# Self-attention: the output projection for two pairs of heads in every odd step, instead of for eight pairs at a batch's end

## The reference

```
def _attn(xq, ctx, wq, wkv, wo, bo):
    q = _heads(xq @ wq)
    k, v = jnp.split(ctx @ wkv, 2, axis=-1)      # then rope on q and k
    sim = jnp.einsum('bhnd,bhmd->bhnm', q, k) * DH ** (-0.5)
    a = jax.nn.softmax(sim, axis=-1)
    o = jnp.einsum('bhnm,bhmd->bhnd', a, v)      # (b, n, 1024) after merging heads
    return o @ wo + bo

attn_in = _adaln(x, cond, ...)
x = _attn(attn_in, attn_in, sa_wq, sa_wkv, sa_wo, sa_bo) + x
x = _attn(_adaln(x, cond, ...), _ln(context, ...), ca_wq, ca_wkv, ca_wo, ca_bo) + x
x = ffn(x) + x
```

## Time and profile before

| | |
|---|---|
| median of 3 runs (lowest, highest) | 1942.67 us (1939.44, 1943.04) |
| profiled execution, its span | 1940.06 us, 1938.3 us |
| PE busy | 1886.2 us, 97% |
| DVE busy | 1573.7 us, 81% |
| POOL busy | 1266.3 us, 65% |
| ACT busy | 945.6 us, 49% |
| self-attention, first to last reciprocal (start) | 43.3 to 404.8 us |

### The profile page before, as it was taken

How to read it: one execution, slowest core, us unless ns; L and a number is a source line. 1 busy time by engine, 2 the same in 40 slices (tenths; PEclk the granted TensorE clock), 3 DMA queues, 4 the chain that set the end, 5 groups by cost and what they waited for, 6 DMA issues and landing times.

```text
span 1938.3 us, 52005 instructions
## 1 busy us (share of the span) xinstructions
PE 1886.2 (97%) x19952; PEld 1288.5 (66%) x19952; DVE 1573.7 (81%) x2292; ACT 945.6 (49%) x1460; POOL 1266.3 (65%) x816
## 2 busy tenths in 40 slices
PE   7989999988999999999999999999999999999999
PEld 5656766755666666666666666666666666666664
DVE  5998888867888888888888888888888888888852
ACT  3445554533544544444554444445544445554444
POOL 5777756415677667666766766776676676767652
PEclk9999999978999999999999999999999999999999
DMA  6322233201111111111111111111111111111110
GB/s 189 105 80 85 78 107 90 78 30 49 59 52 56 51 55 50 56 57 54 56 51 54 52 56 56 54 55 52 53 53 56 56 55 53 54 51 54 50 32 23
DMA packets 147729, 119.07 MB, mean 61 GB/s; under 512 B 63392, under 2 KB 111648, under 8 KB 147488
## 3 DMA queue, kind: packets, MB, share of 16 engines
q1 hardware_dynamic: 110624, 115.46, 17.9%
q10 hardware_dynamic: 36864, 0.28, 1.0%
HBM read 36.71 MB, written 1.05 MB: 19 GB/s over the span
## 4 chain that ended last, share of the span: by engine, by line
PE 86%; issue 3%; DVE 3%; DMA 3%; POOL 2%; SPq 1%; ACT 1%; ACTq 0%; DVEq 0%; POOLq 0%
PE S L1373 24%; PE OB L1387 20%; PE PB L1335 10%; PE PB L1322 9%; PE S L1354 7%; DMA swapped<-turned 2%; PE PB L1396 2%; PE PB L1307 2%; PE S L1224 2%; PE PB L1406 1%; PE PB L1270 1%; PE OB L1252 1%; PE OB L1235 1%; PE PB L1190 1%; DVE QK L966 1%
## 5 line engine op out<-in xcount | busy, mean ns | idle before, releaser
L708 POOL TENSOR_TENSOR psum_acc<-psum_acc,P 124x1024 f32<-124x1024 f32 (+1 forms) x320 | 689.8, 2156 | 214.7 <-ACT P L851 205.2
L851 ACT ACTIVATE P<-S 124x1024 f32<-124x1024 f32 (+1 forms) x448 | 431.3, 963 | 512.4 <-PE S L1373 512.3
L1068 DVE TENSOR_REDUCE mxc<-S 128x2 f32<-128x1024 f32 x384 | 470.0, 1224 | 91.4 <-PE S L1354 84.4
L1387 PE MATMUL OB<-P,V 124*64 124x256 f32 (+1 forms) x3328 | 436.0, 386 | 0.0
L1387 PEld LDWEIGHTS OB<-P,V 124*64 124x64 f32 (+1 forms) x3328 | 221.0, 136 | 187.6 <-issue 103.4
L701 POOL TENSOR_TENSOR psum_acc<-P 124x1024 f32<-124x1024 f32 x64 | 152.0, 2375 | 211.8 <-ACT P L851 208.3
L1373 PE MATMUL S<-QH,KH 64*124 64x256 f32 (+1 forms) x1664 | 272.0, 323 | 5.8 <-ACT P L851 5.8
L728 ACT ACTIVATE V<-PB 124x512 f32<-124x512 f32 (+1 forms) x320 | 157.2, 491 | 203.0 <-PE PB L1335 165.3
L1373 PEld LDWEIGHTS S<-QH,KH 64*124 64x124 f32 (+1 forms) x1664 | 154.1, 181 | 128.2 <-issue 104.3
L1373 PE MATMUL S<-QL,KH 64*124 64x256 f32 (+1 forms) x1664 | 235.1, 278 | 0.0
L1373 PE MATMUL S<-QH,KL 64*124 64x256 f32 (+1 forms) x1664 | 234.8, 278 | 0.0
(11 more groups left out here) (159 smaller groups left out, 2828.7 us busy)
## 6 DMA issues: line engine op xcount, KB each, us to landing
swapped<-turned SPq DMA_DIRECT2D x512, 128.0 KB, 2.1
kv_w<-sa_kv_dram SPq DMA_DIRECT2D x64, 128.0 KB, 2.3
qswapped<-qturned SPq DMA_DIRECT2D x128, 64.0 KB, 1.9
kv_w<-ca_kv_dram SPq DMA_DIRECT2D x64, 96.0 KB, 2.2
ctxT_all<-ctx_dram SPq DMA_DIRECT2D x8, 624.0 KB, 4.6
q_w<-sa_wq_dram SPq DMA_DIRECT2D x64, 64.0 KB, 2.0
q_w<-ca_wq_dram SPq DMA_DIRECT2D x64, 64.0 KB, 1.9
o_w<-ca_wo_dram SPq DMA_DIRECT2D x64, 64.0 KB, 2.0
```

The source lines that it names most:

```text
L708: pool.tensor_tensor(acc, acc, P_of(J, c)[0:rows, :, 0:w], ALU.add).then_inc(x.acc, 1)
L851: act.activation(P_of(J, c)[0:rows, :, 0:w], SP[0:rows, :, 0:w], ACT.Exp, scale=SCALE).then_inc(x.e, 1)
L1068: dve.tensor_reduce(mxc[:, t, :, c:c + 1], MP[:, :, 0:w], AX.X, ALU.max).then_inc(x.am, 1)
L1387: ins = pe.matmul(OB[half(h), 0:N], Vb[J % 2][0:w, t, half(h)], P_of(J, c)[0:w, h, k * N:(k + 1) * N], start=(t == 0), stop=(t == len(a_.t ...
```

## The change

`o` moves to the second place of PE's turn, between `qk` and `p`, and two steps behind instead of one. It now acts in every odd step J, in turn J + 2: four matmuls for the pairs J - 1 and J, as an accumulation of their own. `ad` goes two steps behind too, between `am` and `r`, and adds each such part to `xT`; the bias goes with the first part of a batch. There are 32 groups of 4 matmuls for 8 groups of 16, and 32 additions for 8. The semaphores `z.y` and `z.added` count to 32 instead of 8, and their waits are rewritten; the buffers `oTs` stay eight.

```
-                 "qk+3 ln+3 p+-1 sum+-1 v+2 s a+2 ct o+-1 n",
-                 "c+2 ln+2 am+1 r+2 t+3 rc+-1 dv+-1 ad+-1 cn n",
+                 "qk+3 ln+3 o+-2 p+-1 sum+-1 v+2 s a+2 ct n",
+                 "c+2 ln+2 am+1 ad+-2 r+2 t+3 rc+-1 dv+-1 cn n",
...
                 def divide(J, _):
-                    wait(dve, z.y, batch(J))
+                    wait(dve, z.y, (J - PAIRS) // 2 + 1)
...
                 def add(J, _):
-                    if J % PAIRS == PAIRS - 1:
-                        wait(dve, z.y, batch(J) + 1)
+                    if J % 2:
+                        wait(dve, z.y, J // 2 + 1)
+                        wait(dve, z.added, J // 2)
                         x_b = xT[:, batch(J) * N:batch(J) * N + N]
-                        add_to_x(x_b, XB[:, 0:N], 8).then_inc(z.added, 1)
+                        add_to_x(x_b, XB[:, 0:N], 8 if J % PAIRS == 1 else None).then_inc(z.added, 1)
...
-                           "o": (z.added, lambda K, k: batch(K) + 1 if K % PAIRS == PAIRS - 1 else None)}
+                           "o": (z.added, lambda K, k: K // 2 + 1 if K % 2 else None)}
...
                 def output(J, _):
-                    if J % PAIRS == PAIRS - 1:
-                        wait(pe, z.wo, 16 * PAIRS)
+                    if J % 2:
+                        if J == 1:
+                            wait(pe, z.wo, 16 * PAIRS)
                         wait(pe, z.ot, J + 1)
                         x_free(uses, readers, J, ("o", 0))
-                        for p in range(PAIRS):
+                        for p in (J % PAIRS - 1, J % PAIRS):
                             for h in range(2):
                                 ins = pe.matmul(XB[half(h), 0:N], o_w[p][:, half(h)], oTs[p][:, :],
-                                                start=(p == 0), stop=(p == PAIRS - 1))
+                                                start=(p % 2 == 0), stop=(p % 2 == 1))
                         ins.then_inc(z.y, 1)
```

More of the change, by code:

```diff
@@ L525, in cross_out_weights @@
                 if J < UNROLL:
-                    wait(sp, z.y, B)
+                    wait(sp, z.y, STEPS // 2)
                 sp.dma_start(o_w[r][:, :], packs["ca"][2][pair]).then_inc(x.wo[r], 16)
@@ L1239, in transposes @@
                         wait(pe, z.oe, J)
-                        wait(pe, z.added, 2)
+                        wait(pe, z.added, PAIRS)
                         first[FIRST[J]](0)
@@ L1328, in project_v @@
                     if J == 0:
-                        wait(pe, z.added, B)
+                        wait(pe, z.added, STEPS // 2)
                     x_free(uses, readers, J, ("v", g))
@@ L1419, in ramp_mean @@
                     if k == NLN - 2:
-                        pe.wait_ge(z.added, B)
+                        pe.wait_ge(z.added, STEPS // 2)
                     others["mean"](k)
```

## The result

| | before | changed |
|---|---|---|
| median (lowest, highest; executions) | 1942.59 us (1938.47, 1948.58; 16) | 1935.89 us (1930.89, 1938.40; 16) |
| profiled execution, its span | 1940.06, 1938.3 us | 1936.41, 1934.6 us |
| granted clock, mean over the executions | 0.989 to 0.990 | 0.987 |

The ratio is 0.9963 [0.9954, 0.9972], that is 7.2 us less (5.4 to 8.9). Forecast were 1932.5 us and 10.2 less.

What follows compares the result with a forecast made beforehand. DVE was taken to bound plain steps, PE those with transposes, both losing at batch ends. Terms -31.5 + 3.9 + 1.4 + 8.1 + 6.1 + 1.8 = -10.2 us, from 1942.67, gave 1932.5 us, range 1926 to 1941.

Steps and rivals of the forecast that it cites:

- the sum: Whole change: 31.5 us saved at batch ends, less the added costs of the stretches and turn 63, gives -10.2 us.
- signs of being wrong: Waits of 0.3 us before `v` or sums in many odd turns, fold releasing them, or self-attention gain that cross-attention doesn't keep.
- DVE decides: Steps 0 to 23 and 39 to 46: each odd turn costs 0.34 us for its addition, 3.9 and 1.4 us.
- The cover: Odd turns without transposes: PE's added matmuls are hidden, the sums ending a bare 0.1 us before DVE wants them.
- PE decides: Steps 23 to 39: eight odd turns cost 1.01 us each, 8.1 us against 9.0 saved.
- six paid groups: Steps 46 to 62: six odd-turn matmul groups at 1.01 us each cost 6.1 us against 9.0 saved.
- DVE's idle time: Before the additions: as a sign of being right, it falls from 28.7 us to under 3.
- Turn 63: Last self-attention sums wait for an addition queued behind cross-attention work; scores 2.0 us late, 1.8 us lost.
- The step that failed: Ramp into cross-attention: 12 fewer matmuls, 2.75 us of PE, counted as nothing because PE waits for DVE's maximum anyway.
- rival 2: Ramp: thinner PE work brings TensorE's lower clock some 6 us earlier, costing about 3 us: 1935.5; chance 0.13.
- Rival 3: Odd turns: a PE, DVE, PE round trip stalls each of 31 by 0.84 us, 26 us in all: 1958.5; chance 0.08.
- Rival 4: PE covers it all: transposed turns hide half of their groups and turn 63 costs nothing, 8 us better: 1924.5; chance 0.07.

Runs made afterwards that it cites:

- parity: The changed kernel with the first 16 groups of context transposes starting in turn 23 instead of 24: 1930.89 us, ratio 0.9945.
- The filler: The changed kernel plus twelve matmuls with overwritten results ahead of the ramp's last output group: 1931.53 us, run again 1930.82 us.
- thin_before: The kernel before with twelve of the ramp's sixteen output matmuls left out: 1946.68 us, ratio 1.0016.
- group_only: Against the kernel before: groups of four matmuls with an addition each in odd steps, at the old place: 1969.58 us, ratio 1.0144.
- place_only: Against the kernel before: the batch's 16 matmuls and one addition kept whole, moved to the new place: 1934.87 us, ratio 0.9963.

## Why the prediction was right, and where it was not

The time came out 3.4 us above the forecast and inside its range. Up to the ramp's first scores the sum held, 9.1 and 9.9 us of 10.2, and some of that is luck: steps 46 to 61 gave 1.7 us more than worked out and made up for most of what the other stretches lacked. One of the signs of being wrong came true as well, a gain in self-attention that the run doesn't keep: 2.4 to 2.8 us of it.

*DVE decides (steps 0 to 23, 39 to 46).* The mechanism is right: 5.39 us for an odd turn, predicted and measured, with the wait for the fold gone. The cover was 0.28 us where I had 0.1. Steps 0 to 23 gained 0.9 to 1.4 us less than the sum: 0.9 of it lies between steps 0 and 1 of the first profile, where nothing is changed, and 0.4 to 0.8 in one even step (from step 12 to 13: 5.43 and 5.90 us, 5.06 before). In that step DVE stands idle for 0.27 and 0.75 us ahead of the rotation and PE waits 0.49 and 0.99 us for it; the trace names nothing that released the rotation.

*PE decides (23 to 39).* Odd turns take 6.16 to 6.34 us where 6.3 was predicted, and the gain is 0.5 us for 0.9. One even step, from 36 to 37, that the sum has at no cost takes 6.3 and 6.2 us for 5.3. Again the rotation is late, though no addition stands in this step:

```profile
247.82 0.69 DVE L966 TENSOR_TENSOR QK<-PB,swapped 128x512 f32<-128x512 f32 x1 [1.18 <-issue]
...
248.66 0.66 PE L1201 MATMUL PB<-kv_w,ainT 128*64 128x128 f32 x8 [0.80 <-DVE QK L966]
```

"issue" means that the profile shows nothing that it waited for, so why it is late stays open.

*46 to 62.* Mis-sized: "six paid groups" at 1.01. Turns 51, 55 and 59 paid 0.5 to 0.6 against the same turns before, because the small group of transposes stands at the end of the turn before. `parity` shows it by moving the same gain to the first block, 2.4 us.

*DVE's idle time.* Under 3 us was predicted, 8.9 measured. The prediction's own working has DVE waiting for `o` where PE decides (256.31), so the sign was wrongly chosen: those waits cost nothing beyond the 1.01.

*Turn 63.* The trap was there, 2.07 us of wait where 2.0 was worked out. It costs 1.8 to 2.4 us where I had 1.8.

*The step that failed* is the ramp: "`zo0` shrinks by 12 matmuls, 2.75 us of PE. I count nothing for it." It costs 2.4 to 2.8 us in the profiles, and the time came out at rival 2's price (1935.5 against 1935.9), which I had given 0.13. Its size fits too: some 7 us more at the lower level in the ramp (38 for 31, estimated above) where rival 2 had 6. That the total meets it within 0.4 us is partly luck, since the steps before the ramp gave 0.3 to 1.1 us less than the sum. I had looked at which instruction waited for which, and there the twelve matmuls are indeed hidden; their loss shows in the clock. The filler and `thin_before` show the sign; the size of the ramp's loss rests on one profile of before and two of the change.

Rival 3 fell: no odd turn shows the price of 0.84 us. What it describes is real at the old place, where an odd turn of `group_only` takes 1.36 us more (6.75 for 5.39). Rival 4 fell too: odd turns with four transposes paid about 1.0 us, and turn 63 was not free.

*Open:* why the split was not faster than `place_only` in the medians is explained by the ramp only in size. In the profiles the split gains 4.0 to 4.8 us from the first reciprocal to the ramp's first scores, turn 63 included, and its ramp takes 4.6 to 5.0 us longer than that of `place_only`. And the 2.3 to 2.6 us of the start: the granted clock was 0.50 from 24 to 26 us in both profiles of the changed kernel and 1.00 in the kernel before. It was 0.50 in six of the eleven profiles of kernels with the split and in none of three without it, all with the same program up to that point. I have no run that tells chance from cause.

## What to carry to other kernels

When an accumulation closes between two engines, look first for the place in the order where its inputs are long done and its reader comes late; splitting it at a bad place multiplies the round trip, and at a good place it adds little. Work that is hidden in a thin stretch of TensorE may still hold up its clock, as twelve matmuls did in this ramp (0.9905 for 0.9874 in the mean): before removing it, read the granted clock of the stretch, and judge by many timed executions. The place of an instruction inside a turn decides which turn feels it.

## What was not expected of the hardware

Twelve matmuls whose result is overwritten made the kernel 5 us faster (1930.82 for 1935.96), and twelve fewer made the kernel before 3.1 us slower (ratio 1.0016). One and the same stretch took from 70.8 to 75.8 us in fourteen profiles, by its granted clock of 0.84 down to 0.75. Executions of one program lie up to 12 us apart (before: 1935.92 to 1947.49 in 25), at mean granted clocks of 0.995 down to 0.986.
